# A graph network layer on one core: the output stage gets its bias from TensorE, its rows normalized on ScalarE, its expert weights loaded earlier, another wait between units, and its last chunk in two units

## The reference, cut to what matters

```
a    = attention(h)                    # per node, 8 heads, from the stage before
x2   = x2 + a @ Wo + bo                # projection, bias, residual
t    = (x2 - mean) * rsqrt(var + eps)  # layer norm of each row, no affine part
p    = softmax(mean_over_rows(t) @ Wr + br)          # one router for all rows
e0, e1, share = two best experts after a capacity cut, softmax of the two
y    = t + sum_e share_e * (gelu(t @ W1[e] + b1[e]) @ W2[e] + b2[e])
out  = x2 + layer_norm(y) * gamma + beta
```

## Time and profile before

| | |
|---|---|
| median of 3 runs | 5948.36 us (5946.02 to 5952.58) |
| the profiled execution | 5954.48 us, of which its span 5952.7 us |
| TensorE matmul / VectorE / ScalarE / GpSimd busy | 48% / 77% / 16% / 60% of the span |
| mean granted TensorE clock | 0.826 of full speed |
| output stage, first to last instruction | 5431.72 to 5952.7 us, 9% of the span |

### The profile page before, as it was taken

One profiled execution on the slowest core, in us unless ns is written; L12 is line 12 of the kernel. 1 busy time (PEld: TensorE's weight loads), 2 busy tenths in 40 slices (PEclk: granted clock), 3 DMA queues, 4 the chain that ended last, 5 costly groups with the idle time before them and its releaser, 6 DMA issues. The chain is left out here.

```text
span 5952.7 us, 40357 instructions
## 1 busy us (share of the span) xinstructions
PE 2832.9 (48%) x10552; PEld 1752.9 (29%) x10552; DVE 4609.5 (77%) x9300; ACT 949.1 (16%) x2658; POOL 3597.6 (60%) x3664
## 2 busy tenths in 40 slices
PE   0312332540001008999996444444444444445798
PEld 0212222430001005666664111211111111113565
DVE  7988888779989845566653899999898999987433
ACT  0111111111111113222221111111111111111222
POOL 3777777777777774232202777777777777775000
PEclk9999999999955558999998677776777677777899
DMA  3444444433333331121103888888888888885000
GB/s 86 159 148 151 145 148 155 139 122 105 105 101 105 106 110 42 41 88 60 59 31 106 255 265 261 268 261 266 262 264 265 260 267 261 266 262 160 23 19 19
DMA packets 343617, 924.97 MB, mean 155 GB/s; under 512 B 86388, under 2 KB 126021, under 8 KB 343258
## 3 DMA queue, kind: packets, MB, share of 16 engines
q0 software_dynamic: 201712, 588.31, 33.1%
q1 hardware_dynamic: 98042, 175.20, 8.4%
q10 hardware_dynamic: 43632, 158.88, 6.9%
HBM read 662.53 MB, written 259.59 MB: 155 GB/s over the span
## 5 line engine op out<-in xcount | busy, mean ns | idle before, releaser
L1701 POOL DMA_INDIRECT big<-keys_values,idx x1712 | 1623.0, 948 | 521.7 <-issue 521.7
L592 POOL DMA_INDIRECT big<-in_edge_attr,big x1568 | 1590.9, 1015 | 567.1 <-issue 459.9
L1919 PE MATMUL bank<-big,ident 128*128 128x512 f32 x1712 | 998.1, 748 | 1155.5 <-DVE big L1806 1155.5
L1919 PEld LDWEIGHTS bank<-big,ident 128*128 128x128 f32 x1712 | 407.7, 246 | 1745.4 <-issue 1712.5
L832 DVE SCALAR_TENSOR_TENSOR bank<-bank,big 128x128 f32<-128x128 f32 x1565 | 560.9, 358 | 255.0 <-DMA big<-in_edge_attr,big 205.6
L1796 DVE TENSOR_TENSOR big<-big,bank 128x1024 f32<-128x1024 f32 x428 | 511.7, 1217 | 196.1 <-DMA big<-keys_values,idx 196.1
L904 ACT ACTIVATE big<-bank 128x512 f32<-128x512 f32 x392 | 234.2, 597 | 1851.0 <-DVE bank L832 1834.2
L301 PE MATMUL bank<-ident,big 128*128 128x128 f32 x210 | 51.8, 426 | 996.4 <-DVE big L241 996.4
L1801 DVE TENSOR_REDUCE big<-big 128x32 f32<-128x1024 f32 x428 | 519.2, 1213 | 0.0
L857 PE MATMUL bank<-big 128*128 128x50 bf16 x3200 | 354.9, 278 | 321.0 <-DVE big L646 321.0
L1806 DVE TENSOR_TENSOR big<-big,bank 128x1024 f32<-128x1024 f32 x428 | 500.2, 1212 | 0.0
(11 more groups left out here) (361 smaller groups left out, 4163.8 us busy)
## 6 DMA issues: line engine op xcount, KB each, us to landing
running_sums<-big ACTq DMA_DIRECT2D x196, 512.0 KB, 2.8
running_attention<-big SPq DMA_DIRECT2D x107, 544.0 KB, 4.4
queries_by_row<-big ACTq DMA_DIRECT2D x107, 512.0 KB
big<-queries_by_row SPq DMA_DIRECT2D x107, 512.0 KB, 6.1
big<-keys_values,idx POOLq DMA_INDIRECT x1712, 3.8
big<-in_edge_attr,big POOLq DMA_INDIRECT x1568
keys_values<-big SPq DMA_DIRECT2D x7, 1792.0 KB, 7.4
x_after_layer<-big SPq DMA_DIRECT2D x7, 896.0 KB, 5.8
```

Source lines behind the costliest of these rows:

```text
L592: pool.indirect_dma_start(out=z.rows[:, r, k, :], out_offset=None, in_=w["edge_attr_128"][:, :], in_offset=bass.IndirectOffsetOnAxis(ap=z. ...
L1701: pool.indirect_dma_start(out=kv[:, r, k, :], out_offset=None, in_=t["kv"][:, :], in_offset=bass.IndirectOffsetOnAxis(ap=m.idx2[:, c:c + 1 ...
L1919: mm = pe.matmul(bank[2 * (b % 2) + i // 2][:, :], lhsT=m.ident[:, :], rhs=kv[:, b % RINGK, i * S + j:(i + 1) * S + j + 1:S, D:KW], start= ...
```

## The change

1. **Bias on TensorE.** bo is loaded twice into one partition instead of being broadcast to 128. `add_bias` is gone. In `project` each of the four groups begins with a matmul of a row of ones (1 x 128) by bo (1 x 512, for the last group 1 x 256), and the products accumulate on it.
2. **Rows normalized on ScalarE.** VectorE's `norm` becomes `norm_factors`: the reciprocal, and shift = -mean * rstd (one small instruction). ScalarE does seven activations of 128x256 with a scale and a bias from SBUF, behind its copy of the next attended rows.
3. **Weights loaded at the choice.** gamma and beta are loaded in the first block, after the residual rows. The eight loads of expert weights are issued by SyncE in the first block as soon as `max_index` is done, W1 and b1 of the first expert first. In the second block TensorE does `hidden(0, 0)` and `hidden(0, 1)` as soon as these two are there, ahead of the shares and the mixed b2.
4. **Bank wait apart from statistics.** Between units TensorE does `hidden(u, 0)` and `hidden(u, 1)` and then waits for `f_added` (the additions out of the banks) instead of the statistics. The one-element copy of L933 is gone from this stage.
5. **Last chunk in two.** The last chunk becomes two units of 4 and 3 blocks, each with its own gelus (one of 512 or 384 columns), square root, norm and store.

```diff
-            def add_bias(c):
+            def add_projected(c):
                 dve.wait_ge(s["x2_loaded"], 16 * (c + 1))
-                st.then(v.tensor_tensor(x3[:, c], x3[:, c], bo.unsqueeze(1).to_broadcast([P, CB, D]), ALU.add))
...
-            def norm(c):
+            def norm_factors(c):
                 dve.wait_ge(s["o_norm_deviation"], c + 1)
+                if c:
+                    dve.wait_ge(s["o_tokens_ready"], c)
                 st.then(v.reciprocal(rstd[:, c, :], dev))
-                if c:
-                    dve.wait_ge(s_af, 8 * c + 4)
-                for b in range(CB):
-                    ins = v.tensor_scalar(tok[:, b, :], x3[:, c, b, :], mv[:, c, b, 0:1], rstd[:, c, b:b + 1], ALU.subtract, ALU.mult)
-                ins.then_inc(s["o_tokens_ready"], 1)
+                v.scalar_tensor_tensor(out=shift, in0=mv[:, c, :, 0], scalar=-1.0, in1=rstd[:, c, :], op0=ALU.mult,
+                                       op1=ALU.mult).then_inc(s["o_norm_factors"], 1)
...
+            def norm(c):
+                act.wait_ge(s["o_norm_factors"], c + 1)
+                for b in range(CB):
+                    ins = a(tok[:, b, :], x3[:, c, b, :], ACT.Identity, scale=rstd[:, c, b:b + 1], bias=shift[:, b:b + 1])
+                ins.then_inc(s["o_tokens_ready"], 1)
...
+                    pe.matmul(bk[:, 0:len(blocks) * D], lhsT=m.ones[0:1, :], rhs=bo[0:1, 0:len(blocks)].rearrange("p a d -> p (a d)"),
+                              start=True, stop=False, skip_group_check=True)
...
+            for dst, name in ((gamma, "L1_ffn_gamma"), (beta, "L1_ffn_beta")):
+                sp.dma_start(dst, w[name].unsqueeze(0).to_broadcast([P, D])).then_inc(s["expert_weights"], 16)
+            sp.wait_ge(s["experts_chosen"], 1)
+            for e in range(2):
+                x = sp.value_load(rti[0:1, e:e + 1], min_val=0, max_val=NE - 1)
+                done = s["expert_weights"] if e else s["first_expert_weights"]
+                sp.dma_start(w1[:, e], w["L1_ffn_W1"][bass.ds(x, 1), :, :].rearrange("o (k p) f -> p (o k) f", p=P)
+                             ).then_inc(done, 16)
...
+    units = [(c, 0, CB) for c in range(NC - 1)] + [(NC - 1, 0, 4), (NC - 1, 4, CB)]
...
+            pe.wait_ge(s["first_expert_weights"], 32)
+            hidden(0, 0)
+            hidden(0, 1)
             pe.wait_ge(s["weights_row"], 2)
...
+            for u in range(len(units)):
+                if u:
+                    hidden(u, 0)
+                    hidden(u, 1)
+                    pe.wait_ge(s["f_added"], u)
                 for ef in range(8):
-                    if ef < 7:
-                        hidden(c, ef + 1)
-                    products(c, ef)
+                    if 0 < ef < 7:
+                        hidden(u, ef + 1)
+                    products(u, ef)
```

More of the change, by code:

```diff
@@ L2135, in _ @@
             r.then(v.max(one(7), one(6)))
-            r.then(v.max_index(rti[0:1, :], one(7), one(6)))
+            v.max_index(rti[0:1, :], one(7), one(6)).then_inc(s["experts_chosen"], 1)
+            dve.wait_ge(s["experts_chosen"], 1)
             softmax(7, 8, 2)
@@ L2285, in _ @@
             st = Steps(dve, s["f_steps"])
-            def chunk(c, first=False):
-                xc = x3[:, c]
-                for b in range(CB):
-                    st.add(v.tensor_scalar(tok[:, b, :], xc[:, b, :], mv[:, c, b, 0:1], rstd[:, c, b:b + 1], ALU.subtract, ALU.mult))
-                st.wait()
-                st.then(v.tensor_tensor(tok, tok, b2s.unsqueeze(1).to_broadcast([P, CB, D]), ALU.add))
-                dve.wait_ge(s["f_products"], c + 1)
-                for k in range(4):
-                    e = min(2 * k + 2, CB)
-                    part = tok[:, 2 * k:e, :].rearrange("p b d -> p (b d)")
-                    st.add(v.tensor_tensor(part, part, bank[4 + k][:, 0:(e - 2 * k) * D], ALU.add))
-                st.wait()
-                row_norm(dve, s["f_norm_stats"], s["f_norm_deviation"], st, v, m, tok, normed, bn, late_mv, late_rstd, None, c + 1)
-                st.then(v.tensor_tensor(normed, normed, gamma.unsqueeze(1).to_broadcast([P, CB, D]), ALU.mult))
-                st.then(v.tensor_tensor(normed, normed, beta.unsqueeze(1).to_broadcast([P, CB, D]), ALU.add))
-                if not first:
-                    dve.wait_ge(s["y_stored"], c * 16)
-                v.tensor_tensor(y, normed, xc, ALU.add).then_inc(s["y_ready"], 1)
@@ L2309, in _ @@
+            for u, (c, lo, hi) in enumerate(units):
+                unit(u, c, lo, hi)
         @block.scalar
@@ L2326, in _, with hidden @@
         def _(pe):
+            def hidden(u, ef):
+                c, lo, hi = units[u]
+                if ef >= 2:
+                    pe.wait_ge(s["f_gelu"], u * 8 + ef - 1)
+                e, f = ef // 4, ef % 4
+                for h, cols in enumerate(columns(lo, hi)):
+                    for k in range(2):
+                        mm = pe.matmul(bank[2 * (ef % 2) + h][:, 0:cols.stop - cols.start], lhsT=w1[:, e, k, f * P:(f + 1) * P],
+                                       rhs=tT_all[:, c, k, cols], start=(k == 0), stop=(k == 1))
+                mm.then_inc(s["f_hidden"], 1)
@@ new lines, in products @@
+            def products(u, ef):
+                c, lo, hi = units[u]
+                pe.wait_ge(s["f_gelu"], u * 8 + ef + 1)
+                for i, b in enumerate(range(lo, hi)):
+                    mm = pe.matmul(bank[4 + i // 2][:, (i % 2) * D:(i % 2 + 1) * D], lhsT=hT[:, ef % 2, b * P:(b + 1) * P],
+                                   rhs=w2[:, ef // 4, ef % 4, :], start=(ef == 0 and i % 2 == 0), stop=(ef == 7), skip_group_check=True)
+                mm.then_inc(s["f_rows"], 1)
+            pe.wait_ge(s["first_expert_weights"], 32)
```

168 lines of the change are left out of this document (87 added, 81 removed).

## The result

The changed kernel took 5992.44 us (median of 4 runs, 5984.61 to 6001.17) against 5949.80 us for the kernel before (4 runs, 5946.02 to 5952.58). The ratio is 1.0070, 95% interval 1.0058 to 1.0082: 43 us slower. The forecast was 5954.5 us, no measurable change, with a range from 5941 to 5963.

What follows compares the result with a forecast made beforehand. It took a ring through TensorE, VectorE and ScalarE to bound the projection and TensorE to pace feed-forward. Its terms summed to +6.1 us, applied to the median of 5948.36: 5954.5 us, range 5941 to 5963.

Steps and rivals of the forecast that it cites:

- The clock in the projection (-2.7): Projection: with the new period one to two of six chunks start at 2.4 GHz instead of 1.2, -2.7 us.
- The bias on TensorE (+19.8): Projection: four added matmuls lengthen each chunk's ring, while the removed VectorE addition returns nothing, +19.8 us.
- Rival A: Projection: TensorE's clock stays low twice as long in each chunk, +18.7 us in all, 5967 us; chance 0.12.
- B: Projection: the one-row bias costs TensorE almost nothing, -11 us in all, 5937 us; chance 0.07.
- C: Feed-forward boundaries: they gain their whole idle time, 14.8 us instead of 1.2, 5941 us; chance 0.06.
- D: Projection: a function table load in every chunk on ScalarE, up to +9 us, 5963.5 us; chance 0.04.
- E: Projection: the clock stays up in all chunks, -7.2 us more, 5947.3 us; chance 0.09.
- Rows on ScalarE (+1.2): Projection: ScalarE's seven activations are hidden except in the last chunk, where they take longer than VectorE's normalization, +1.2 us.
- Weights at the choice (-5.6): From written index to first products: earlier weight loads and hidden pair bring the products forward, -5.6 us.
- Bank wait (-1.2): Feed-forward boundaries: products still wait for root, table load and gelu, so only the removed copy is gained, -1.2 us.
- Last chunk in two (+3.4 and -7.4): End of feed-forward: the extra boundary stalls TensorE, +3.4 us, and the work after the last products shrinks, -7.4 us.
- Last stores (-1.4): Final store: 256 KB instead of 768 KB go ahead of the last rows, -1.4 us.

Runs made afterwards that it cites:

- bias_128_rows: The changed kernel with the operands of its bias matmuls made of 128 rows instead of one: 5964.87 us, ratio 1.0021 against the kernel before.
- bias_on_vector: The changed kernel with the bias addition and its broadcast load back on VectorE, all other parts kept: 5943.00 us, ratio 0.9989 against the kernel before.
- gelu_first: bias_on_vector with ScalarE taking a unit's square root only behind the next unit's first two gelus: 5919.57 us, ratio 0.9943 against the kernel before.
- bias_alone: The kernel before with only part 1 of the change, the one-row bias on TensorE: 5999.83 us, ratio 1.0080 against the kernel before.
- bias_64_rows: The changed kernel with a bias operand of 64 rows instead of one: 5991.71 us against 5957.49 for the kernel before.
- bias_grouped: The changed kernel with the one-row bias matmuls of the first three groups issued together at the chunk's head: 5998.22 us beside 5946.46 for the kernel before.

## Why the prediction was wrong

**The clock in the projection (-2.7), the step that failed.** "The new rhythm has the same gap but another period, so I expect one to two of the six chunks to start at 2.4 GHz". Two of the six did (those at 5492.27 and 5529.78), but the four others were low for 7 to 17 us instead of about 3, and the effect as a whole had the other sign. Of the 28.3 us by which one row makes the projection longer than 128 rows do, some 18 are TensorE's lower clock. My range took from the clock only a gain as its good end and nothing as its bad end, though no one-row matmul of 512 columns stood in any row.

**The bias on TensorE (+19.8).** Right for an operand of 128 rows: the groups are 2.58 us apart, the 0.86 + 1.72 of the working (1.72 for eight products), and the projection came out at 114.6 us, +18.9 where the three terms had +18.3. For the operand of one row the term lacks some 10 us of pauses, for which the prediction has no term at all. Rows 4 had led me to "no discount that the trace knows". They say that for the mean duration of one matmul, and such a mean holds records at both clocks. A timeline of the same trace would have shown both effects. The 98 records of 8 rows lie in seven groups of 14 between matmuls of 128 rows, in a stage in which TensorE is dense. The first three lines are the group at 2539.95 and its neighbours, the last two the weight loads at the group of 2405.38:

```profile
2533.85 6.18 PE L1442 MATMUL bank<-big 128*128 128x448 f32 x16
2539.95 4.13 PE L1433 MATMUL bank<-big 8*128 8x256 f32 x14
2544.01 8.80 PE L1453 MATMUL bank<-big 128*128 128x256 f32 x28
```

```profile
2405.38 2.88 PEld L1433 LDWEIGHTS bank<-big 8*128 8x128 f32 x14 [0.65 <-issue]
2408.59 7.60 PEld L1453 LDWEIGHTS bank<-big 128*128 128x128 f32 x28 [0.33 <-issue]
```

Fourteen records of 256 columns take 3.0 us at 2.4 GHz. This group's span is 4.06 us and the 28 records behind it take 8.80 where they take 6.21 elsewhere: the clock fell to 1.2 GHz at 2542.3, within the group, though TensorE had not been idle since 2424.9. It fell within the group, or within 0.6 us of its end, at all seven in the kernel before, and at five of the seven in the changed kernel's trace. And the gaps of 0.65 and 0.33 us in the weight loads are those of the one-row operand: from start to start, the two switches at 2405.38 and 2408.59 cost 0.39 us, as in the projection.

**Rival A** had the clock's mechanism (low for longer, slower than before) at a chance of 0.12, but it priced one more low stretch of the length seen before, 1.65 us a chunk, and gave 5967 us. Low stretches were up to 17 us long (chunk at 5467.76), and cost 18 / 7 = 2.6 us a chunk on average beyond those of `bias_128_rows`. It also gave the period of the loop as its reason, and not the rows. B, C, D and E did not happen: at 2.4 GHz the one-row pair costs a group 2.97 - 1.72 = 1.25 us; the boundary gained almost nothing; the projection has the one table load ahead of its first root (5445.90) that it had before (5450.92) and no other; the clock did not stay up.

**Rows on ScalarE (+1.2).** 1.4 us from the aggregation to the transposes (4.4 us against 3.0). Seven activations took 3.55 us:

```profile
5585.28 3.55 ACT L2200 ACTIVATE big<-big 128x256 f32<-128x256 f32 x7 [0.47 <-DVE big L2116]
```

0.51 us each, where I had 0.45 from the rows. An estimate from the Trainium skill (ScalarE: Activation LUTs, What ACT_TABLE_LOAD costs) gives 3.5 us and +1.5; the trace, with 3.55 and 1.4, agrees with it more than with my estimate. And by the Trainium skill (the same page, Table sets: the hidden batching unit) rival D could not occur, which this trace agrees with too.

**Weights at the choice (-5.6).** -7.5, at the good end of its bounds, and partly luck. All engines indeed met after SyncE's last issue (5604.46, block start 5604.90). The clock rose early in the hidden pair (7.65 us instead of 8.58) and did not fall after it in this execution, which I had given two chances in three. In the profiles of the fourteen other runs with this code it fell, which costs 1.5 us in the first products of `bias_on_vector`; that loss is counted there among the products, where the changed kernel has none.

**Bank wait (-1.2).** Right in mechanism and size: chunk to chunk 51.24 us against 51.34, and 0.7 at the last boundary. `gelu_first` shows that the root's place on ScalarE was the bound.

**Last chunk in two (+3.4 and -7.4).** The end was right (-7.3). The boundary was mis-sized: the stall was 6.05 us, as worked out (5.97), but the 2.58 of the second unit's hidden pair should not have been taken off. Before, both hidden groups of the whole chunk lay inside the previous boundary's stall already, so nothing was saved. To this came 1.7 us for products at the low clock (3.44 us for 8 records, then 1.73), behind 4.46 us in which TensorE idles: the first unit's hidden pair is shorter than a full chunk's.

**Last stores (-1.4).** -1.5.

**Not in the prediction:** the first transposes, which wait for gathered rows, came 1.8 us later. The same stretch was long in `bias_alone` (17.3 us) and somewhat longer than before in `bias_128_rows` (16.5), but not in `bias_64_rows` and `bias_grouped` (15.2 each), though all of them load bo twice. Its cause is open. It is 5% of the loss.

## What to carry to other kernels

A small matmul that "only adds a bias" costs its columns and, with 64 rows or fewer among full ones, pauses at each switch and the clock of the loop around it, as measured here in float32: give it all 128 rows (which still cost 22 us here, `bias_128_rows` against `bias_on_vector`), or leave the addition where it is hidden. Before an engine is relieved, find the ring that sets the period: VectorE was busy 13.10 of the 13.61 us of a chunk in the kernel before, and relieving it returned nothing until the ring was cut by reordering. A mean duration of a group mixes both clocks and hides what happens at its edges: before a shape is called free, read a timeline of one place where it stands. A wait that is removed in front of another wait only changes its name; look at what the same engines wait for next, function table loads included.

## What the runs showed of the hardware that I had not expected

In all kernels of this case TensorE treats a float32 matmul of 64 rows or fewer (1, 8, 32 and 64 were measured) differently from one of 65 or 128, in two ways. Its granted clock is low for longer when such matmuls stand in a dense loop: six chunks took 121 to 123 us with 1 or 32 rows, 115 with 64, 101 with 65 and 100 with 128, and 101 with 128 rows of which 127 hold zeros. TensorE shows as busy without a gap in the low stretches (2.00 of 2.00 us in the window at 5476.00), and in the kernel before the clock fell behind over 100 us without an idle gap, within 14 records of 8 rows (at 2542.3). And next to full matmuls it pauses: the weight load after such a matmul isn't taken ahead, which costs 0.39 us for the two switches of a group at 2.4 GHz. Busy times hide these pauses (the records of a group add up to 1.12 + 1.99 us and overlap); they are seen only by the distances between the starts of groups. With the same idle time ahead of them (2.46 us), the boundaries of feed-forward kept the clock in the kernel before and lost it four times of six in `bias_alone`. The cause of the step at 65 rows inside the engine stays open.
